# Fourier mode mix of a spectral network: one half of the images mixed inside the other half's pass

## What is computed

```python
def _spectral_conv(x, w1, w2):
    xf = jnp.fft.rfft2(x).reshape(Bb, G, WID, Hh, Wf)
    lo = jnp.einsum('bgixy,gioxy->bgoxy', xf[:, :, :, :M1, :M2], w1c)
    hi = jnp.einsum('bgixy,gioxy->bgoxy', xf[:, :, :, Hh - M1:, :M2], w2c)
    ...
    return jnp.fft.irfft2(out_ft.reshape(Bb, G * WID, Hh, Wf), s=(Hh, Ww))
...
h = _gconv1x1(h, fc0_w, fc0_b)
for i in range(4):
    h1 = _spectral_conv(h, sp_w1[i], sp_w2[i])
    h2 = _gconv1x1(h, w_w[i], w_b[i])
    h = h1 + h2
    if i < 3:
        h = _gswish(h, betas[i])
h = _gswish(_gconv1x1(h, fc1_w, fc1_b), betas[3])
return _gconv1x1(h, fc2_w, fc2_b)
```

## Time and profile before

| | |
|---|---|
| median of 3 runs | 3428.85 us (3423.66 to 3441.11) |
| the profiled execution | 3424.0 us, its span 3422.0 us |
| mean granted TensorE clock | 0.92 |
| PE busy | 2749.5 us (80%) |
| DVE busy | 1898.7 us (55%) |
| ACT busy | 1432.5 us (42%) |
| POOL busy | 748.6 us (22%) |

### The profile page before, as it was taken

One profiled execution on the slowest core, in us unless ns is written; L12 is line 12 of the kernel. 1 busy time (PEld: TensorE's weight loads), 2 busy tenths in 40 slices (PEclk: granted clock), 3 DMA queues, 4 the chain that ended last, 5 costly groups with the idle time before them and its releaser, 6 DMA issues. The chain is left out here.

```text
span 3422.0 us, 44205 instructions
## 1 busy us (share of the span) xinstructions
PE 2749.5 (80%) x17124; PEld 2137.0 (62%) x17124; DVE 1898.7 (55%) x2438; ACT 1432.5 (42%) x2409; POOL 748.6 (22%) x675
## 2 busy tenths in 40 slices
PE   0699996869485299579996899779996699999658
PEld 0244443436253298579895798669985687887535
DVE  6988776735625311245544455355453478878643
ACT  1777775722122122253334333253333466666322
POOL 3988501213110000000000000000000044444310
PEclk9999998989797699789997999889998899999879
DMA  8300006679334566868676676758767634332134
GB/s 206 68 24 0 24 6 164 187 153 203 96 92 132 105 139 143 220 156 203 160 175 202 151 200 160 182 151 190 194 166 185 119 59 85 59 63 49 63 90 95
DMA packets 344001, 438.03 MB, mean 128 GB/s; under 512 B 260422, under 2 KB 302022, under 8 KB 317406
## 3 DMA queue, kind: packets, MB, share of 16 engines
q1 hardware_dynamic: 343319, 430.43, 52.4%
q0 software_dynamic: 496, 5.01, 0.4%
HBM read 258.62 MB, written 168.58 MB: 125 GB/s over the span
## 5 line engine op out<-in xcount | busy, mean ns | idle before, releaser
L1061 DVE STREAM_TRANSPOSE spec_chan<-spec_form_in 128x1024 f32<-128x1024 f32 x256 | 491.7, 1945 | 63.2 <-PE fno_pz L1277 63.2
L1363 ACT ACTIVATE fno_act<-fno_pz 128x320 f32<-128x320 f32 x512 | 223.8, 437 | 616.2 <-PE fno_pz L1277 616.2
L1252 POOL TENSOR_SCALAR fno_minus<-fno_both 96x960 f32<-96x960 f32 x32 | 83.4, 2606 | 1376.7 <-DVE fno_both L1455 1376.7
L1447 DVE COPY fno_wfreq<-fno_pw 128x240 f32<-128x240 f32 x256 | 97.7, 395 | 513.5 <-PE fno_pw L1305 511.5
L1277 PEld LDWEIGHTS fno_pz<-spec_cols,spec_chan 128*128 128x128 f32 x3072 | 348.2, 192 | 12.3 <-issue 9.5
L1277 PE MATMUL fno_pz<-spec_cols,spec_chan 128*128 128x96 f32 x3072 | 350.0, 275 | 2.0 <-ACT spec_cols L1371 2.0
L1328 PE MATMUL fno_pz<-fno_act,fno_wt 128*40 128x64 f32 x2304 | 205.8, 264 | 148.2 <-DMA fno_act<-scratch_modes 107.7
L1581 POOL TENSOR_TENSOR head_hact_lo<-head_hact,head_hact_hi 128x512 fp32r<-128x512 f32 x128 | 227.9, 1783 | 400.7 <-DVE head_hact_hi L1728 400.7
L1305 PE MATMUL fno_pw<-fno_fw,fno_act 128*128 128x96 f32 x2560 | 303.4, 277 | 14.4 <-DVE fno_wfreq L1447 8.6
L1305 PEld LDWEIGHTS fno_pw<-fno_fw,fno_act 128*128 128x128 f32 x2560 | 291.4, 192 | 26.9 <-DVE fno_wfreq L1447 15.4
L1328 PEld LDWEIGHTS fno_pz<-fno_act,fno_wt 128*40 128x40 f32 x2304 | 198.8, 140 | 157.7 <-issue 143.5
(11 more groups left out here) (173 smaller groups left out, 4806.0 us busy)
## 6 DMA issues: line engine op xcount, KB each, us to landing
scratch_form<-fno_act SPq DMA_DIRECT2D x32, 2560.0 KB, 17.2
spec_form_in<-scratch_form SPq DMA_DIRECT2D x64, 1024.0 KB
fno_act<-scratch_modes SPq DMA_DIRECT2D x128, 180.0 KB
nca_raw<-scratch_xnp SPq DMA_DIRECT2D x66, 329.7 KB
fno_coef<-scratch_mixed SPq DMA_DIRECT2D x48, 360.0 KB, 10.9
spec_form_in<-scratch_form SPq DMA_DIRECT2D x32, 512.0 KB
fno_wt<-table_mix_w SPq DMA_DIRECT2D x32, 450.0 KB, 11.1
gn_x<-scratch_x SPq DMA_DIRECT2D x12, 1024.0 KB
```

Source lines behind the costliest of these rows:

```text
L1061: return nc.vector.transpose(chan[:, to * TR * PIX:(to + 1) * TR * PIX].rearrange("p (h q w) -> p h q w", h=TR, q=4), src)
L1363: nc.scalar.activation(act_b[:, n % 2, :, 4 * t:4 * t + 4], z, ACT.Silu if layer else ACT.Copy).then_inc(a_out, 1)
```

## The change

The images are now mixed in two halves of 4 units (a side: q = 0 to 7 through the 4 layers). `mixed_in(n)` places the 24 mix tiles of a side, one for each kx row, in the second and third unit of the other half's pass, 12 in each unit, one behind each `pointwise` tile from the fourth on. Only the last side, of the last layer, is mixed after the passes. A mix tile is 12 matmuls that move 32 columns (16 images) past 40 weight columns. It writes to the two banks that `inverse_rows` uses (`pj`), and `pj_free` waits for whoever empties them. The modes loaded and the six result tiles in flight have their own buffers, and `act_b` shrinks from two buffers to one. The mixing weights are loaded once for each side. Mixed tiles are stored by DMAs that ACT issues. Modes are stored, and coefficients loaded, for two units at a time. The fill of `cols` between layers is done by POOL and ACT in place of a DMA.

The core of the diff ("..." where lines are left out):

```diff
@@ -1039,12 +1039,11 @@
-XC = 3
+XC = 2
 CHUNKS = NX // XC
-TILES = 2 * XC
-F = 2 * KY
-HT = TILES // 2
-WTS, XB = 4, 4
+XB, OB = 3, 6
+PER, MIX_AT = NX // 2, 3
+FH = B * KY // 2
...
-        act_b = ph.sb("act", [128, 2, CS, H])
+        act_b = ph.sb("act", [128, CS, H])
         wfreq = ph.sb("wfreq", [128, 2, 20 * SB])
-        both, minus = ph.sb("both", [4 * NX, 20 * SB]), ph.sb("minus", [4 * NX, 20 * SB])
-        coef = ph.sb("coef", [4 * NX, CH // 2, 2 * SB])
+        both, minus = (ph.sb(n, [4 * NX, 20, 2, SB]) for n in ("both", "minus"))
+        coef = ph.sb("coef", [4 * NX, CH // 2, 2, 2 * SB])
         fw, fh = ph.sb("fw", [128, 2 * SB]), ph.sb("fh", [128, 2, 4 * NX])
         wz = ph.sb("wz", [128, 96])
-        om1 = ph.sb("om", [CH, XC * 4 * B * KY])
-        wt = ph.sb("wt", [128, WTS, XC * KY, CH])
+        xm = ph.sb("xm", [128, XB, XC, 2, FH])
+        om = ph.sb("om", [CH, OB, 2, 2 * FH])
+        wt = ph.sb("wt", [128, XB, XC * KY, CH])
...
+        def mixed_in(n):
+            q = n // 4 - 1
+            return range(q * NX + PER * (n % 4 - 1), q * NX + PER * (n % 4)) if q >= 0 and n % 4 in (1, 2) else range(0)
+
+        last_mix = range((SIDES - 1) * NX, SIDES * NX)
...
+                def load_modes(c):
+                    if c >= XB:
+                        sp.wait_ge(mix_done, (c - XB + 1) * XC)
+                    x, f = c % CHUNKS * XC, c // CHUNKS % 2 * FH
...
+                def store_modes(pair):
+                    sp.wait_ge(d_out, 2 * (pair + 1) * NH)
+                    sp.wait_ge(m_out, 2 * (pair + 1))
...
+                for n in range(ALL):
+                    layer, u = n // UNITS, n % UNITS
+                    if n % 4 == 0 and n:
+                        begin_mix(n // 4 - 1)
+                    if n % 4 == 2:
+                        store_modes(n // 2 - 1)
+                    for m in mixed_in(n):
+                        feed_mix(m)
+                    sp.wait_ge(a_out, (n + 1) * NZ)
+                    if n:
+                        sp.wait_ge(act_stored, 16 * n)
+                    sp.dma_start(form[layer % 2, u], act_b[:, :, :].rearrange("p c h -> p (c h)")).then_inc(act_stored, 16)
+                    if n % 4 == 0 and n:
+                        first_modes(n // 4 - 1)
...
+                    if u == UNITS - 1:
+                        pool.wait_ge(scaled, LAYERS)
+                        pool.wait_ge(set_up, 2)
+                        pool.wait_ge(z_done, (n + 1) * NZ)
+                        nc.gpsimd.tensor_copy(cols[:, 0:COLS // 2].rearrange("p (h c) -> p h c", c=CS), wide(wsm[:, layer, :], H // 2, 1)).then_inc(fill_pool, 1)
...
+                def pj_free(user):
+                    i = pj_at[user] - 2
+                    if i >= 0:
+                        kind, m = pj_users[i]
+                        if kind == "rows":
+                            pe.wait_ge(j_out, m + 1)
+                        else:
+                            pe.wait_ge(out_s if m % 2 else out_v, m // 2 + 1)
...
+                    c = m // XC
+                    if m % XC == 0:
+                        pe.wait_ge(wt_in[c % XB], 16 * (c // XB + 1))
+                        pe.wait_ge(x_in[c % XB], 64 * (c // XB + 1))
+                    pj_free(("mix", m))
+                    rows = xm[:, c % XB, m % XC, :, :].rearrange("p r (a y b) -> p r a y b", y=KY, b=B2)
+                    for y in range(KY):
+                        mm = nc.tensor.matmul(pj[0:CH, pj_at["mix", m] % 2, y * 32:(y + 1) * 32], wt[:, c % XB, m % XC * KY + y, :],
+                                              rows[:, :, :, y, :], start=y == 0, stop=True, skip_group_check=True)
+                    mm.then_inc(mix_done, 1)
+
+                for n in range(ALL):
+                    for t in range(NZ):
+                        if t == 2 and n:
+                            forward_rows(n - 1)
+                        pointwise(n, t)
+                        if len(mixed_in(n)) and MIX_AT <= t < MIX_AT + PER:
+                            mix(mixed_in(n)[t - MIX_AT])
+                    if UNITS <= n + 1 < ALL:
+                        inverse_rows(n + 1 - UNITS)
+                    forward_cols(n)
+                forward_rows(ALL - 1)
+                for m in last_mix:
+                    mix(m)
...
+                def activate(n, t):
                     act.wait_ge(z_done, n * NZ + t + 1)
-                    if t == 0 and n >= 2:
-                        act.wait_ge(w_done, (n - 1) * NW)
-                        act.wait_ge(act_stored[n % 2], 16 * (n // 2))
+                    if t == 0 and n:
+                        act.wait_ge(w_done, n * NW)
+                        act.wait_ge(act_stored, 16 * n)
...
+                def mix_out(m):
+                    act.wait_ge(mix_done, m + 1)
+                    if m >= OB:
+                        act.wait_ge(stored[m % OB], 16 * (m // OB))
+                    layer = m // (2 * NX)
+                    for ri, v, part, sign in PARTS:
+                        op = nc.scalar.activation(om_tile(m, ri, v), acc_tile(m, part), ACT.Copy,
+                                                  scale=rates[0:CH, 2 if sign > 0 else 3, 1, layer:layer + 1])
+                    op.then_inc(out_s, 1)
+
+                def store_mixed(m):
+                    act.wait_ge(out_s if m % 2 else out_v, m // 2 + 1)
+                    f = m // NX % 2 * 2 * FH
+                    act.dma_start(mixed[:, m % NX, :, f:f + 2 * FH].rearrange("r c f -> c r f"), om[:, m % OB, :, :]).then_inc(stored[m % OB], 16)
+
+                for n in range(ALL):
+                    for t in range(NZ):
+                        activate(n, t)
+                        if len(mixed_in(n)) and MIX_AT <= t < MIX_AT + PER and (t - MIX_AT) % 2:
+                            m = mixed_in(n)[t - MIX_AT]
+                            mix_out(m)
+                            if t - MIX_AT > 1:
+                                store_mixed(m - 3)
+                                store_mixed(m - 2)
+                    for m in mixed_in(n)[-2:]:
...
+                        act.wait_ge(scaled, LAYERS)
+                        act.wait_ge(z_done, (n + 1) * NZ)
+                        nc.scalar.activation(cols[:, COLS // 2:COLS].rearrange("p (h c) -> p h c", c=CS), wide(wsm[:, n // UNITS, :], H // 2, 1), ACT.Copy).then_inc(fill_act, 1)
+                        act.wait_ge(fill_act, n // UNITS + 1)
+                        act.wait_ge(fill_pool, n // UNITS + 1)
+                    if UNITS <= n + 1 < ALL:
+                        cols_out(n + 1 - UNITS)
...
+                for n in range(ALL):
+                    if n:
+                        row_spectra(n - 1)
+                    outs = mixed_in(n)[0::2]
+                    for e in range(4):
+                        if n >= UNITS:
+                            turn(n, 4 + e)
+                        if len(outs) and e < 3:
+                            mix_out(outs[e])
+                    for m in outs[3:]:
+                        mix_out(m)
...
-                    sp.wait_ge(z_done, (layer + 1) * UNITS * NZ)
-                    sp.wait_ge(scaled, LAYERS)
-                    sp.dma_start(cols[SB:128, 0:COLS].rearrange("p (h c) -> p h c", h=H), wide(wsm[SB:128, layer, :], H, 1)).then_inc(filled, 16)
-                    sp.wait_ge(both_out, (layer + 1) * UNITS * 64)
```

More of the change, by code:

```diff
@@ L1119, in om @@
[L1119 to L1129 removed]
+        blank, blank_half, mix_blank = (ph.sem(n) for n in ("blank", "blank_half", "mix_blank"))
@@ L1241, in _ @@
+                begin_mix(SIDES - 1)
+                first_modes(SIDES - 1)
+                for m in last_mix:
+                    feed_mix(m)
+                for b in range(OB):
+                    sp.wait_ge(stored[b], 16 * NX // OB * SIDES)
+                sp.wait_ge(act_stored, 16 * ALL)
                 sp.wait_ge(iw_in, 64)
@@ L1333, in _ @@
-                for layer in range(LAYERS):
-                    if layer:
-                        inverse_rows(layer, 0)
-                    for u in range(UNITS):
-                        for t in range(NZ):
-                            if t == 2 and u:
-                                forward_rows(layer * UNITS + u - 1)
-                            pointwise(layer, u, t)
-                        if layer and u < UNITS - 1:
-                            inverse_rows(layer, u + 1)
-                        forward_cols(layer * UNITS + u)
-                    forward_rows(layer * UNITS + UNITS - 1)
-                    pe.wait_ge(a_out, (layer + 1) * UNITS * NZ)
-                    for n in range(CHUNKS):
-                        mix(layer * CHUNKS + n)
+                    c = m // XC
@@ new lines, in _ @@
+                for n in range(ALL):
+                    if n:
[7 more added lines that the diff above has]
+                    for m in outs[3:]:
+                        mix_out(m)
+                    for t in range(NW):
+                        column_spectra(n, t)
```

(2 more changed lines are left out.)

321 lines of the change are left out of this document (129 added, 192 removed).

## The result

The changed kernel takes 3410.22 us (median of 15 runs, 3385.84 to 3420.5), the kernel before 3428.85 us (15 runs): a ratio of 0.993, with an interval of 0.9913 to 0.9948. It is faster by some 19 us. I forecast 3449 us and slower. The profiled execution has a span of 3411.2 us (before 3422.0).

What follows compares the result with a forecast made beforehand. PE was taken to bound the passes, with idle time only at the layer boundaries. The terms -321.7 + 322.6 + 22 + 11 + 4 - 12.8 - 4.9 gave +20 us, so 3449 us on the median; range 3360 to 3530 us.

Steps and rivals of the forecast that it cites:

- What it adds to PE: Mix matmuls inside the passes: 4032 records of 32 columns at 80 ns each add 322.6 us.
- rival 2: A mix matmul costs its columns only: at 40 ns PE gets 161 us, kernel 3288 us; chance 0.10.
- Rivals 3 and 4: Mixing units: the clock falls, 3531 us, chance 0.13; data come late, 3 us lost in each, 3491 us, chance 0.07.
- What costs nothing: In the passes, DVE's mix output, ACT's stores and SP's mode loads ahead of `load_unit` were taken to add no time.
- Removed boundaries and the fill: Three layer boundaries: all but `inverse_rows` goes, -321.7 us; filling `cols` by POOL and ACT costs +4 us.
- Ends of the mixing units: PE waits there while ACT empties the last mix tile, issues DMAs, activates and copies: +22 us, bounds 0 to 40.
- One activation buffer: In layer 0 the next activation waits for the store of `form`; PE waits 2.2 us in five units, +11 us.
- Last boundary: The mix after the last layer's passes: 73.7 us in place of 86.5, -12.8 us.
- Start: DVE's memset of the weight buffer goes behind the memsets that the first loads wait for: -4.9 us.

Runs made afterwards that it cites:

- the kernel with four buffers: The changed kernel with four chunk buffers for modes and weights in place of three: 3301.41 us, ratio 0.9628.
- the experiment: Against the kernel with four chunk buffers, SyncE issues a side's first coefficient load ahead of the unit's load instead of behind it: 3306.44 us, ratio 0.9647.

## Why the prediction was wrong

**The step that failed** is the pace of a record in "What it adds to PE". I took 80 ns, "because the two clock levels show a floor under this very instruction". There was no such floor: the 80 ns were 32 pairs being read, and 16 pairs take 40. The reasoning at half clock was sound (the columns bind at 107 ns, and in a row they cost 56 at the full clock, where I had worked out 54); the error was to name what came on top a cost for each pair of instructions when it was the reading of its pieces. The 4032 records inside passes take 161 us at the full clock and not 322.6. That the reading doesn't follow the clock, 115 ns at both levels for single elements, is why 80 ns at the one level and 107 at the other looked like a floor. This is rival 2, to which I gave 0.10 with the right condition, "unless the floor seen there is the reading of the moving operand". Its 3288 us is nearly what the kernel with four buffers takes, 3301, in part by terms that offset one another (the list below).

**What hid it.** Rivals 3 and 4 came true as one, each with the chance of a thing by itself: data late in half of the units, and a clock that falls on the wait and doesn't come back while the work stays mixed (of 51 such falls in all traces, two ended before the mixing did). "What costs nothing" had looked at the loads ahead of `load_unit`, and not at the feed of weights behind the store of the modes, and I had priced a wait at what it lasts. The waits for weights are 22.4 us; all 14 mixing units together take 822.6 us in the changed kernel and 706.8 with four buffers (from a unit's first pointwise tile to the next unit's). The difference is 115.8 us: the waits and eight falls, one of them behind the pause that no wait explains. The same 14 units of the kernel before, which mix nothing, take 490.8. The mixing therefore adds 331.9 us as the kernel stands and 216.0 without falls. That the first is near my 322.6 + 22 is luck: a pace twice too dear against falls that I had left out.

**The terms of the sum,** on the profiled executions, predicted and measured:

- *Removed boundaries and the fill*: from the first pointwise tile of a layer's last unit to that of the next layer's second, the three boundaries lose 105.3, 101.1 and 100.9 us, 307.2 together. Predicted 321.7 - 4 = 317.7. The rest is a new wait of 9.5 us for `fno_coef` at the first of them, which I hadn't named: its load stands behind a unit's load on SyncE, and the experiment shows that they only trade places.
- *Ends of the mixing units*: PE's waits for ACT there are 4.6 us at L1330 and 4.5 at L1315, all units together; predicted 22. What lies between 14 x 24 x 12 x 0.040 = 161 and 216.0 us is mostly the change between two kinds of matmul: 24 records at 40 ns and 8 at 112 make 1.86 us, a step is 2.13; 0.27 x 168 = 45 us. That had no term.
- *One activation buffer*: predicted +11, measured 0: layer 0's units are 27.2 us as before, since the store of `form` now lands in 9.4 us instead of 17.2. I read the old landing as the store's own. It was its place behind the unit's load, and the diff moves it ahead. The term's mechanism is right where that order is kept, and far too small there, because the waits also take the clock and mixed tiles come free late.
- *Last boundary*: from the last unit's first pointwise tile to the head 133.8 us before and 106.7 after, -27.1; predicted -12.8. The mix goes at 67 ns a record at half clock, under the 94 that I took.
- *Start*: the stage's first load (`fno_wz`) is issued at 1127.3 in both kernels, the first pointwise tile comes at 1173.06 and 1161.49: -11.6, predicted -4.9. The first load of images is issued 6.1 us sooner (memset gone from ahead of it); the rest fits with the four loads of weights that were issued right behind `point_w` and are gone, which no run tried alone. From that first load to the first pointwise tile it is 45.3 to 46.3 us in the three kernels with the old start and 34.1 to 36.5 in the nine with the new one.

The sum of these is -307.2 + 331.9 - 27.1 - 11.6 = -14 us, against -10.8 between the two spans, where I had +20. Of the 34 us between, 13 are the mixing, in which a pace twice too dear stands against falls and a change of kind that had no term; 32 are the activation buffer, the last boundary and the start, each taken too dear; and 10 go the other way, at the first boundary. So the sign came out wrong by the small terms as much as by the pace, whose error the falls nearly cancelled.

Open are what makes the instructions late in the pause within a tile, if it is that, and why the clock fell behind some stops and not behind others as long.

## What to carry to other kernels

The pace of a short matmul belongs to its operand's layout as much as to its columns: before scaling one, look at how many pieces the moving operand is read in, and time it once in a row. When work is spread into a dense stream, count the buffers ahead of the engine against the longest hold on the queue that fills them; where the stream's own density doesn't bring the clock back, a wait of 3 us can cost far more behind it than it lasts (here 11 us where half of the mixing was still to come, 6 where two tiles were), which the sum of the waits doesn't show. And a landing time in a trace is that of its place in the queues; when a change reorders the issues around a transfer, neither its old latency nor that of its neighbours stands.

## What the runs showed of the hardware

For a record of these fp32 matmuls with 40 columns of weights, from start to start: 64 columns in a row 56 ns, in pairs 80, as single elements 115, at the full clock; 32 columns in pairs 40, in a row 38. At half clock it is 107 for 64 columns in a row or in pairs, still 115 as single elements, and 67 for 32. I hadn't expected that the clock, once at half, stays there for 21 us in which TensorE is busy 21.07 of 21.10 us, with the same tiles in the same order that hold the full clock when nothing interrupted them. The prediction took the density of the work as what decides; the state from which it starts decides as well.
